# Routing steps of layers 1 to 3 reordered, and layer 1's output norm worked in pairs of tiles beside its output product

## The reference, cut to what matters

```python
for layer in (0, 1, 2, 3):
    xn = layernorm(x)
    x = x + gnn(xn, edges) + mix(xn)
    x = x + ffn(layernorm(x))         # top 2 of 8 experts
# layer 1's mixer ends
out = out @ w_out + b_out
return out / max(norm(out), 1e-12) * out_norm_w * sqrt(512)
# layer 1's gates: softmax(relu(x @ gw1 + gb1) @ gw2 + gb2), top 2, softmax over the two
```

## Time and profile before

| | us |
|---|---|
| median of 3 runs (3089.37 to 3092.78) | 3092.68 |
| the profiled execution | 3084.43 |
| its span | 3082.7 |
| PE busy | 2687.0 (87%) |
| DVE busy | 1705.9 (55%) |
| ACT busy | 1106.4 (36%) |
| POOL busy | 1196.3 (39%) |
| mean granted PE clock | 0.931 |

### The profile page before, as it was taken

One profiled execution on the slowest core, in us unless ns is written; L12 is line 12 of the kernel. 1 busy time (PEld: TensorE's weight loads), 2 busy tenths in 40 slices (PEclk: granted clock), 3 DMA queues, 4 the chain that ended last, 5 costly groups with the idle time before them and its releaser, 6 DMA issues. The chain is left out here.

```text
span 3082.7 us, 46251 instructions
## 1 busy us (share of the span) xinstructions
PE 2687.0 (87%) x16981; PEld 1746.4 (57%) x16981; DVE 1705.9 (55%) x3462; ACT 1106.4 (36%) x2477; POOL 1196.3 (39%) x1445
## 2 busy tenths in 40 slices
PE   7999889999989999999989938999599868499684
PEld 4655668556567756545545626777256645255462
DVE  8876778635678844666526263222435566541644
ACT  3254457332547532322313214444322235310142
POOL 2021677785377778844213121111013136200042
PEclk9999899999989999999999968999899989799897
DMA  2001345432154433424101019999401169500198
GB/s 65 0 21 64 112 144 162 130 123 86 36 153 149 160 115 119 127 76 113 38 11 45 14 55 381 417 416 412 117 14 43 51 224 327 168 14 0 36 381 270
DMA packets 163940, 415.34 MB, mean 135 GB/s; under 512 B 23931, under 2 KB 75675, under 8 KB 140236
## 3 DMA queue, kind: packets, MB, share of 16 engines
q1 hardware_dynamic: 149213, 362.10, 34.3%
q0 software_dynamic: 12960, 42.48, 3.6%
q10 hardware_dynamic: 1555, 7.95, 1.0%
HBM read 325.37 MB, written 87.09 MB: 134 GB/s over the span
## 5 line engine op out<-in xcount | busy, mean ns | idle before, releaser
L522 PE MATMUL ps<-units,ARENA 128*125 128x512 f16 x2880 | 640.7, 384 | 15.5 <-POOL units L2743 9.8
L2739 POOL TENSOR_SCALAR raw<-raw 128x512 f32<-128x512 f32 x368 | 258.8, 703 | 885.6 <-PE ps L504 331.4
L504 PE MATMUL ps<-ARENA,units 128*128 128x500 f16 (+1 forms) x2952 | 544.8, 347 | 22.6 <-ACT tmp L1447 6.0
L522 PEld LDWEIGHTS ps<-units,ARENA 128*125 128x125 f16 x2880 | 389.9, 138 | 251.4 <-DVE X L2450 16.5
L504 PEld LDWEIGHTS ps<-ARENA,units 128*128 128x128 f16 x2952 | 291.6, 99 | 273.9 <-issue 27.2
L1856 DVE TENSOR_TENSOR ARENA<-tmp,ARENA 128x500 f16<-128x500 f32 (+3 forms) x229 | 161.4, 710 | 368.6 <-ACT ARENA L1373 182.7
L2743 POOL TENSOR_TENSOR AT<-raw,AT 128x512 f16<-128x512 f32 x200 | 242.3, 1211 | 17.0
L2787 POOL DMA_INDIRECT ARENA<-rows_d,proj x81 | 80.3, 991 | 385.6 <-DVE ARENA L2256 359.6
L2743 POOL TENSOR_TENSOR units<-raw,units 128x512 f16<-128x512 f32 x180 | 219.6, 1220 | 15.3
L2792 POOL DMA_INDIRECT picks_d<-ARENA,proj x81 | 81.9, 1011 | 348.4 <-DVE ARENA L2296 347.6
L1372 ACT ACTIVATE tmp<-ps,cols 128x500 f32<-128x500 f32 (+1 forms) x144 | 87.6, 608 | 355.1 <-PE ps L504 348.1
(11 more groups left out here) (461 smaller groups left out, 4468.3 us busy)
## 6 DMA issues: line engine op xcount, KB each, us to landing
ARENA<-split_d SPq DMA_DIRECT2D x135, 1024.0 KB
raw<-in_moe SPq DMA_DIRECT2D x200, 256.0 KB, 3.0
split_d<-AT SPq DMA_DIRECT2D x200, 256.0 KB, 2.5
raw<-in_units SPq DMA_DIRECT2D x180, 256.0 KB, 2.5
ARENA<-split_d SPq DMA_DIRECT2D x27, 1280.0 KB
rows_d<-ARENA SPq DMA_DIRECT2D x6, 896.0 KB
ARENA<-picks_d SPq DMA_DIRECT2D x6, 896.0 KB
ARENA<-picks_d ACTq DMA_DIRECT2D x6, 896.0 KB
```

What stands on the lines that cost most here:

```text
L504: ins = pe.matmul(o[:, 0:nt * R], wt, mv_, start=(i == 0), stop=(i == len(steps) - 1))
L522: ins = pe.matmul(o[0:R, :], th(srcT, h, k, t, 1), w(k, g), start=(i == 0), stop=(i == len(steps) - 1))
L2739: pool.tensor_scalar(r, r, WEIGHT_SCALE, gain, ALU.mult, ALU.mult).then_inc(sem("pool_step"), 1)
```

## The change

Layer 1's output norm: the twelve groups of transposes are no longer behind a whole layer norm. DVE's `output_by_pairs` evicts tile t and then scales, adds and takes statistics of tile t-2; the norms are rooted and inverted by pairs of tiles. The factor sqrt(512) moves into the root. The normalising itself moves to ACT (`norm_rows`), for chunk 0 before the squares of tile 6; its transposes and halves come before tile 8 of the product (`beside_direct`).

Routing: first_row and end_row are counted in rows from the start (tri8 and tile_row hold multiples of B), the expert of each tile is worked out before the one-hot tables, a shift and a scaling are gone, two products are one. `slots` writes gather_i straight from PSUM and signals it first. The split of the expert rows moves from `expert_rows` to the wait for the gate's bank. Layer 1's logits are read with their bias in one step.

```diff
@@ -1211,14 +1210,15 @@
                 uses_row()
                 if mem:
                     uses_row()
-                gemm_N("K", lambda k, g: w[:, g, k, :], "att_out")
+                gemm_N("K", lambda k, g: w[:, g, k, :], "att_out", between=beside_direct if mem else None)
                 free(u, "dve")
 
 
             linear_attention(1)
 
 
-            transposes_T(lambda t, a, b: nat(Y, t, a, b), "y", "lo_D")
+            direct_columns(1)
+            direct_columns(2)
             pe.wait_ge(*loaded())
             u, w = unit()
             gemm_T([(w, "YT", 4)], "gateT", n_oc=2, direct=True)
@@ -1733,17 +1733,25 @@
                 evac_direct("K", "k")
                 if mem:
                     for t in range(T):
+                        if t == 6:
+                            norm_rows(0, X)
+                        if t == 8:
+                            evac_direct("YT", groups=(0, 4))
                         act.wait_ge(sem("att_out"), s.more("att_out", 1))
                         ins = act.activation(nat(M, t), nat(Y, t), ACT.Square, accum_out=small[0:R, 32 + t:33 + t])
-                    ins.then_inc(sem("act_step"), s.one("act_step"))
-                    act.wait_ge(*s.latest())
-                    roots(T, small[0:R, 32:32 + T], 0.0, p=R)
+                        if t % 2 == 1:
+                            ins.then_inc(sem("act_step"), s.one("act_step"))
+                            act.wait_ge(*s.latest())
+                            roots(2, small[0:R, 31 + t:33 + t], 0.0, scale=1.0 / D, dst=std[0:R, t - 1:t + 1])
 
 
             linear_attention(1)
 
-            ln_root()
-            evac_direct("YT")
+            norm_rows(1, X)
+            evac_direct("YT", groups=(4, 7))
+            norm_rows(2, X)
+            marks[1] = ("normed", s.sent["normed"])
+            evac_direct("YT", groups=(7, 12))
             for k in range(2):
                 for t0, nt in CH:
                     evac("act", "gateT", tr(Q, k, t0, nt), nt * R, ACT.Relu, col("L1gb1", k), WS)
@@ -2218,30 +2226,27 @@
                 step(dve.tensor_reduce(n_tiles, over, AX_X, ALU.add))
                 before = over80[:, 0:NE * NE].rearrange("p (e f) -> p e f", f=NE)
                 step(tt(before, n_tiles.unsqueeze(1).to_broadcast([128, NE, NE]), tri8, ALU.mult))
-                step(dve.tensor_reduce(first_tile, before, AX_X, ALU.add))
-                step(tt(end_tile, first_tile, n_tiles, ALU.add))
-                step(ts(first_row, first_tile[0:R, :], float(B), None, ALU.mult))
-                step(tt(slot_pos.rearrange("p (t e) -> p t e", e=NE), o[0:R, 0:T * NE].rearrange("p (t e) -> p t e", e=NE),
-                        first_row.unsqueeze(1).to_broadcast([R, T, NE]), ALU.add), "read_dve")
-                for k in range(2):
-                    ins = tt(picked[:, k * 80:(k + 1) * 80], slot_pos, K[0:R, (3 + k) * T * NE:(4 + k) * T * NE], ALU.mult)
-                step(ins)
+                step(dve.tensor_reduce(first_row, before, AX_X, ALU.add))
+                tt(slot_pos.rearrange("p (t e) -> p t e", e=NE), o[0:R, 0:T * NE].rearrange("p (t e) -> p t e", e=NE),
+                   first_row[0:R].unsqueeze(1).to_broadcast([R, T, NE]), ALU.add).then_inc(sem("read_dve"), s.one("read_dve"))
+                step(stt(end_row, n_tiles, float(B), first_row, ALU.mult, ALU.add))
+                step(tt(le_scratch, end_row.unsqueeze(1).to_broadcast([128, TILES, NE]), tile_row.unsqueeze(2).to_broadcast([128, TILES, NE]), ALU.is_le))
+                step(dve.tensor_reduce(expert_of, le_scratch, AX_X, ALU.add))
+                step(ts(expert_of, expert_of, float(NE - 1), None, ALU.min))
+                step(dve.tensor_copy(expert_i, expert_of), "tile_experts")
+                step(tt(picked.rearrange("p (k c) -> p k c", k=2), slot_pos.unsqueeze(1).to_broadcast([R, 2, T * NE]),
+                        K[0:R, 3 * T * NE:5 * T * NE].rearrange("p (k c) -> p k c", k=2), ALU.mult))
                 step(dve.tensor_reduce(pos20, picked.rearrange("p (i e) -> p i e", e=NE), AX_X, ALU.add))
                 step(dve.tensor_copy(pos_i.bitcast(I32), pos20))
-                step(ts(tile_i.bitcast(I32), pos_i.bitcast(I32), 7, None, ALU.logical_shift_right))
                 step(ts(part_i.bitcast(I32), pos_i.bitcast(I32), B - 1, None, ALU.bitwise_and))
-                step(dve.tensor_copy(tile_f, tile_i.bitcast(I32)))
                 step(dve.tensor_copy(part_f, part_i.bitcast(I32)))
+                step(stt(tile_f, part_f, -1.0, pos20, ALU.mult, ALU.add))
                 for i in range(2 * T):
                     ts(on_part[:, i, :], iota128[0:R, :], part_f[:, i:i + 1], None, ALU.is_equal)
-                step(tt(on_equal, tile_f.unsqueeze(2).to_broadcast([R, 2 * T, TILES]), iota27[0:R, :].unsqueeze(1).to_broadcast([R, 2 * T, TILES]), ALU.is_equal))
+                step(tt(on_equal, tile_f.unsqueeze(2).to_broadcast([R, 2 * T, TILES]), tile_row[0:R, :].unsqueeze(1).to_broadcast([R, 2 * T, TILES]), ALU.is_equal))
                 for k in range(2):
                     ins = tt(on_tile[:, k * T:(k + 1) * T, :], on_equal[:, k * T:(k + 1) * T, :], tok1[0:R, :].unsqueeze(2).to_broadcast([R, T, TILES]), ALU.mult)
                 step(ins, "routing_step")
-                step(tt(le_scratch, end_tile.unsqueeze(1).to_broadcast([128, TILES, NE]), iota27.unsqueeze(2).to_broadcast([128, TILES, NE]), ALU.is_le))
-                step(dve.tensor_reduce(expert_of, le_scratch, AX_X, ALU.add))
-                step(ts(expert_of, expert_of, float(NE - 1), None, ALU.min))
-                step(dve.tensor_copy(expert_i, expert_of), "tile_experts")
 
             def slots():
 
@@ -2250,10 +2255,10 @@
                     dve.wait_ge(*s.latest())
                 dve.wait_ge(sem("filled_dve"), s.more("filled_dve"))
                 o = s.bank("dve")
+                step(ts(gather_i, o[:, 0:TILES], -1.0, 0.0, ALU.add, ALU.max), "slots")
                 step(dve.tensor_copy(slot_sb, o[:, 0:TILES]), "read_dve")
-                step(ts(gather_i, slot_sb, -1.0, 0.0, ALU.add, ALU.max))
                 step(stt(slot_z, slot_sb, 0.0, pad_rows, ALU.is_equal, ALU.mult))
-                step(stt(slot_sb, slot_sb, -1.0, slot_z, ALU.add, ALU.add), "slots")
+                step(stt(slot_sb, slot_sb, -1.0, slot_z, ALU.add, ALU.add))
                 dve.memset(on_w[:, 0:T, 2, :], 0.0)
                 dve.tensor_copy(on_w[:, T:2 * T, 2, :], on_equal[:, T:2 * T, :])
                 step(dve.tensor_copy(w_hi, w_picks))
...
@@ -2273,6 +2278,12 @@
                 step(ts(slot[0:40], slot[0:40], WEIGHT_SCALE, None, ALU.mult))
                 step(dve.tensor_copy(expert_rows16[0:40, :], slot[0:40]))
                 step(tt(expert_rows16[32:40, :], slot[32:40], expert_rows16[32:40, :], ALU.subtract))
+
+            def expert_rows(name):
+
+                def step(ins, name="dve_step"):
+                    ins.then_inc(sem(name), s.one(name))
+                    dve.wait_ge(*s.latest())
                 row_free(name)
                 step(ts(tile_row16, expert_of[0:40, :], row_expert[0:40, :], None, ALU.is_equal), "routing_step")
                 dve.wait_ge(sem("filled_dve"), s.more("filled_dve"))
@@ -2379,18 +2390,18 @@
                 for e in range(NE):
                     ins = dve.memset(rev[:, :, e:e + 1], float(NE - e))
                 step(ins)
+                if pair_softmax:
+                    expert_rows_in_parts(pair_softmax)
                 dve.wait_ge(sem("filled_dve"), s.more("filled_dve"))
                 o = s.bank("dve")
                 if gbias:
-                    step(dve.tensor_copy(lg, o[0:R, 0:T * 8].rearrange("p (t e) -> p t e", e=NE)), "read_dve")
+                    b = row("gb2")
+                    step(tt(lg, o[0:R, 0:T * 8].rearrange("p (t e) -> p t e", e=NE), b[:, 0:NE].unsqueeze(1).to_broadcast([R, T, NE]), ALU.add), "read_dve")
+                    row_free("gb2")
                 else:
                     parts = o[0:R, 0:T * 16].rearrange("p (t g e) -> p t g e", g=2, e=NE)
                     step(ts(lg, parts[:, :, 0, :], WS, None, ALU.mult))
                     step(stt(lg, parts[:, :, 1, :], WS, lg, ALU.mult, ALU.add), "read_dve")
-                if gbias:
-                    b = row("gb2")
-                    step(tt(lg, lg, b[:, 0:NE].unsqueeze(1).to_broadcast([R, T, NE]), ALU.add))
-                    row_free("gb2")
                 if probs:
@@ -2582,40 +2593,63 @@
                     ts(bd[0:64, hp * 128:hp * 128 + 64], o[0:64, 0:64], small[0:64, 8 + hp:9 + hp], None, ALU.mult)
                     ts(bd[64:128, hp * 128 + 64:hp * 128 + 128], o[64:128, 64:128], small[64:128, 8 + hp:9 + hp], None, ALU.mult).then_inc(sem("ctx2"), s.one("ctx2"))
                 low_direct("K", "k")
-                b = row("L1bout" if mem else "L2bout")
+                if mem:
+                    output_by_pairs()
+                    return
+                b = row("L2bout")
```

(68 more changed lines are left out.)

11 lines of the change are left out of this document (6 added, 5 removed).

## The result

| | median, us | runs | ratio to before, 95% interval |
|---|---|---|---|
| before, first series | 3092.7 | 4 | |
| after, first series | 3065.5 (3063.5 to 3067.2) | 4 | 0.9915 (0.9893 to 0.9936) |
| before, second series | 3090.7 (3085.9 to 3095.8) | 11 | |
| after, second series | 3071.7 (3065.7 to 3075.6) | 6 | 0.9936 (0.9924 to 0.9949) |

3064 was forecast, 3052 to 3078 as the range. The first series gives 27.3 us less than before, the second 19.0 less; the forecast was 28.5 less. So the time came out as forecast, while the difference is about 20 us by the second, larger series. The two intervals overlap, so 27.3 and 19.0 us are not shown to differ. The question is which terms of the sum are too large.

The account below looks back on a forecast made before the run. PE binds most stages but waits 26.1 us for DVE's layer norm in layer 1 and for the routing's gathers. Gains 16 + 0.5 + 4.4 + 4.0 + 3.6 = 28.5 take the median from 3092.7 to 3064 us, range 3052 to 3078.

Parts of the forecast that it names:

- output norm: Layer 1, output product to gateT: norm work run inside the product starts gateT 16 us earlier, bounds 10 and 20.
- gates: Layer 1's logits take one operation in place of two, 0.5 us; splitting the expert rows earlier costs nothing.
- layer 1's routing: Earlier loads let layer 1's second gather land sooner, sharing only their last 3 us: 4.4 us, bounds 0.3 and 6.
- layer 2's: Layer 2's routing: first gather lands earlier, PE then held only by slot_weights: 4.0 us, bounds 0.3 and 5.
- layer 3's: Layer 3's routing: DMA-bound, so the third load's earlier start counts: 3.6 us, bounds 0.3 and 5.
- full blocking: Rival in layer 1's output norm: GpSimd blocks DVE, leaving 7 of 16 us, 3073; chance 0.04.
- the hole costs the clock: Rival at tile 8 of layer 1's output product: last two tiles and gateT's start at 1.2 GHz, 3070; chance 0.09.
- The slower clock in layer 1's experts: Rival: denser start lowers the mean clock grant to 0.90 over layer 1's experts, 34 us longer, 3098; chance 0.03.
- the gather's time is its own: Rival in the routing: a gather takes 6 to 9 us regardless, each layer gains 0.3, total 17.4, 3075; chance 0.18.

Follow-up runs that it names:

- routing_only: The kernel before with only the new order of the routing's steps, output norm as before: 3082.9 us, ratio 0.9967.
- norm_only: The kernel before with only the output norm by pairs of tiles, routing in its old order: 3081.0 us, ratio 0.9964.
- transposes_behind: The changed kernel with all transposes of layer 1's normed rows behind the output product, none inside it: 3070.4 us, ratio 0.9917.
- two_loads_layer1: The changed kernel with two early expert weight loads in layer 1 in place of four: 3066.4 us, ratio 0.9920.
- four_loads_again: The changed kernel with four early loads in layer 3 in place of two, run a second time for its trace: 3068.0 us in one run.
- loads_behind_gathers: The changed kernel with every expert weight load of all three layers held until the second gather has landed: 3080.1 us, ratio 0.9964.
- loads_late: The changed kernel with the four tile-expert operations back behind the slot mapping, so each layer's first loads start later: 3073.2 us, ratio 0.9929.

## Why the prediction was right, and which terms were not

Redone, the working has one slip in its range: with all upper bounds (20, 0.5, 6, 5 and 5) the sum gives 3056, not 3052. Against the traces, with all terms in us. Layers 2 and 3 vary by 4 to 5 us between traces, so their terms are means: layer 2's old order 178.9 (two traces), its new order 174.4 with early loads (nine traces, 172.9 to 177.1); layer 3's old order 129.5 (two), the new one with two early loads 127.9 (seven, 126.2 to 131.1).

| term | forecast | measured |
|---|---|---|
| output norm | 16 (10 to 20) | 14.7 at gateT's start, 13.1 at bank 1 with the gates |
| gates | 0.5 | 0.3 (28.10 to 27.83 in `routing_only`) to 0.6 (30.22 in `norm_only` to 29.67) |
| layer 1's routing | 4.4 (0.3 to 6) | 1.4 (0.3 against `norm_only`'s 331.35, 2.5 in `routing_only`) |
| layer 2's | 4.0 (0.3 to 5) | 4.5 |
| layer 3's | 3.6 (0.3 to 5) | 1.6, within the spread |
| sum | 28.5 | 20.6 |

**Norm: right in mechanism, a little too large.** 53.5 us lay inside the 50 to 54 given. VectorE's tail went as counted: closing of the first chunk at 1767.1 (1768.4 forecast), one table load, VectorE slowed beside GpSimd by some 2 us (most of it three adds of 1.52, 0.98 and 0.98 in place of 0.69), where 3.5 had been allowed; the full blocking that would have left 7 of the 16 did not occur. PE's stop between tiles 7 and 8 was counted, too: 8.1 us by the forecast (1767.5 to 1775.6), 7.3 measured, with 3.4 us of wait ahead of the four transposes where 3 to 5 were given. What makes gateT 1.5 us later than forecast (53.5 behind the product's start, 52.0) is small and in several places: VectorE's adds take 0.69 in place of 0.61, the last chunk's closing takes 0.9 longer than counted, and VectorE waits 1.8 us in all for ScalarE's high halves, which the sum had at nothing; 1.2 us less for GpSimd and shorter evictions give part of it back. VectorE's idleness at tile 8, 3.5 us where 3 were counted, was a price that another order saves: `transposes_behind` gives 3.7 back. The rival "the hole costs the clock" came true to some 4 us of clock (2.4 in tiles 8 and 9, 1.6 in gateT). On the path lie gateT's 1.6, for which the sum had nothing, and most of tile 8's: its bank came 5.1 us after the tile's start, 2.9 at full clock before, and VectorE stood idle for it. The sum had 1.6 for that. The rival gave 3070.

**Layer 1: the step that failed.** I had the gathers share only the last 3 us of the four loads. The loads did start 4.3 us behind the bank, as said, but the queues moved only from about 2 us later (147 GB/s from 1834 to 1835, 344 in the next), which the sum left out. They ran at some 400 GB/s until 1847, and PE's transposes start at 1847.4: the first gather landed at 1847.3, the last of the four loads at 1847.8. The Trainium skill says in "DMA: Bandwidth & Descriptors", section "Queues, rings and completion order", that each engine serves its queue rows in turn, packet by packet. If that holds here, where the profile has gathers and loads in queues of their own (q0 and q1), one would expect a gather so much smaller than the loads to be through well before them; the trace has it land with them instead, and no run shows why. Besides, PE had been held by the second gather before, with the first tile's copies in its shadow; now both arrive together and 2.6 us of transposes and copies show. `two_loads_layer1` shows that the loads in flight were the cost: 6.5 us less than before in place of 1.4. The 1.4 itself is uncertain, since the clock rises at another place in the first tile's products (0.73 of granted clock over them in the changed kernel, 0.92 in `routing_only`, whose stage is 1.2 us shorter).

**Layer 2: right**, with its floor. PE's slot_weights end, not the gather, sets its first transposes 14.5 us behind the bank (14.5 also with no loads at all; in `four_loads_again` alone, 15.4, where the gather landed at 15.3).

**Layer 3: too large.** I took it for bound by its load stream from the first load on. The third load came 4.1 us earlier behind the bank (15.6, 19.7 before), yet 1.6 arrived at the end, with traces of the new order 5 us apart. `loads_behind_gathers` starts the first load 11 us later but the third only 3.5 (19.1 behind the bank), and loses 2.8. What an earlier stream is worth at the end is therefore not settled. Why the rate of the settled stage differs (3.8 to 4.0 us a tile between traces) is open: what the queues moved differs, at the same share.

**What paid in the routing.** I put it on earlier loads. By `loads_late` they are worth at most some 2 us in layer 2, within the spread, and nothing that shows elsewhere. The rest comes with the other edits, which `loads_late` keeps, the gathers' issue 1.3 us earlier behind the bank among them: its median is 17.5 us below before, that of `norm_only` 10.9. No run has one of them alone. In layer 1 what counts is how many loads lie ahead of the gathers: with four the stage takes 331.1 us, with none 331.1 as well, since PE then waits for weights, and with two, which land before the second gather is issued, 326.0.

**The slower clock in layer 1's experts** did not come: the last scatters but two lie 11.40 us apart (2132.02 and 2143.42), as before.

The sum was 8 too large. That the time was met within 1.5 us all the same is luck: the four runs of the first series lie 6.2 us below the six of the second (3071.7, which is inside the range as well). By its number alone the second series, 19.0 less, lies nearer to the 17.4 of the rival "the gather's time is its own" than to 28.5, though `loads_behind_gathers` refutes that rival's mechanism.

## What to carry to other kernels

A small transfer on which a stage starts should be issued with as little as possible in flight ahead of it: in layer 1, four large loads that began 7 us earlier gained 0.3 to 2.5 us, because they lay between it and its landing. But holding all of them back gained nothing either; two, which were through in time, gained 5.1. When work is put inside a product on another engine, follow each bank it takes to the instruction that frees it, and what stands ahead of that one in its queue. And price an edit by the stages between fixed rows: the stages of layer 1 up to its bank repeat to 0.1 us here between traces of one kernel, those of layers 2 and 3 to some 3 to 5, while executions of one kernel lie 10 to 20 us apart.

## What the runs showed of the hardware

- An indirect gather of 128 rows landed 3.5 us after its issue with no loads in flight (`loads_behind_gathers`, layer 1), and 8.0 us after it with four loads of 1 MB begun ahead of it (the changed kernel).
- The clock's phase costs as much as an edit. Layer 2's mixer, the same code in all traces, took 303.3 to 309.3 us; in its gate products alone 4.1 us lay between 0.93 and 0.50 of granted clock. Over all traces, the mixer took 303.3 to 306.3 us where the clock rose within them (five) and 306.2 to 309.3 where it stayed at 0.50 (eight).
- DMA queues at a share of 0.99 to 1.02 moved 362 GB/s in one execution and 408 in another over 40 us of the same stage; two traces of one kernel had 408 and 385. No run here shows the reason.
